# Logits of a graph network on Trainium2: the six steps of a narrow matmul dealt to four column groups

## The chip, the cores and the metric

The kernel runs on one core of one Trainium2 chip. The metric is the device time of one execution in microseconds, the median of several runs. TensorE (PE) does matmuls, VectorE (DVE) and ScalarE (ACT) work elementwise and empty PSUM, GpSimd (POOL) and SyncE (SP) mostly issue DMAs.

## What is computed

Four layers of a graph network over 512 nodes with 768 features and 8704 edges. Each layer adds a message-passing part, a mixing attention and a feed-forward part to the node features. Two kinds of stage matter here. The attention over edges needs, for each node, relation and head, two numbers (a query and a key logit):

```python
def rgat_conv(x, W, q, k, b, src, dst, etype, heads, out_ch, n_nodes):
    xr = jnp.einsum('nd,rdf->rnf', x, W)
    oi = xr[etype, dst]
    oj = xr[etype, src]
    qi = oi @ q
    kj = oj @ k
    alpha = jax.nn.leaky_relu(qi + kj, NEG_SLOPE)
    ...
```

with 3 relations, and 4 heads in the first of two such layers and 1 in the second; the last layer has an attention of 12 heads and one relation. The expert layers choose one of 8 experts for each node, by the largest of `_layernorm(x) @ Ws + bs`.

## The kernel before

Activations lie transposed: six chunks `[128 features, 512 nodes]` in SBUF, f32. A matmul contracts over 128 features, so that a product over 768 features is six steps (`KC = 6`) that accumulate in one PSUM bank. For the logits the stationary operand is narrow: `logit_w[heads]` has `2 * heads` columns (8, 2 or 24), and the gate of an expert layer 8 (`ME`). The result is `[2 * heads, 512]` in rows 0 up.

Every engine's program is written out by hand, in the order in which its queue runs. The engines meet by semaphores. PSUM's banks 0 to 3 form a ring: `open_bank` on TensorE waits until ScalarE (or VectorE) has emptied the bank four uses back, ScalarE empties the banks in the order in which they were filled (`filled`), and ticks `bank_free`. So a step that is moved on TensorE is moved on ScalarE too.

The stages around the change:

- `rgat` (TensorE, from L1200; ScalarE, from L1925; VectorE, from L2680), called for two layers, three relations each. For a relation: `linear` (36 matmuls with the relation's weights), `edge_logits` (the six narrow steps; ScalarE evicts them to `qkrow`, L1894), `to_tokens` (24 transposes of 128 x 128, six banks, evicted at L1578), `logit_columns` (four small transposes of `qkrow`), and `edge_softmax_row`, which spreads a key row over 128 partitions by a matmul with `key_of`. That last matmul waits for VectorE's `split_keys` (L2669 to L2676, five operations), which splits the f32 keys into three bf16 parts. ScalarE then adds query and key (L1920). For the third relation `to_tokens` comes after all of this, and the first exponentials (L1941) wait for VectorE's row maximum over all three relations.
- `graph_attention` (L1332): the six steps are followed by `res(0)`, which waits for the normalised features (`ln6`, L2282), then `logit_columns` and two rows.
- `experts_of_one` (L990, twice): the six steps of the gate run on the centred, not yet scaled features, behind the sum of squares. ScalarE evicts `logit_rows` (L1810), VectorE multiplies them by `rstd` (L2476, `logit_x`), behind its reciprocal (L2276), and four matmuls with an identity turn them into columns.

`stat` is a small scratch tile, `ident` the 128 x 128 identity.

## Time and profile before

| | |
|---|---|
| median of 3 runs | 4366.4 us (4365.52 to 4368.17) |
| the profiled execution | 4363.68 us, its span 4362.0 us |
| mean granted TensorE clock | 0.981 |
| busy: PE, DVE, ACT | 4137.1, 1153.9, 951.3 us |

The profile shows one execution. A TensorE instruction stands in two rows, PE (the matmul) and PEld (the load of its stationary operand). An f32 matmul is two records of each. A timeline row merges equal instructions: start, duration from the first start to the last end, count, and in brackets how long the engine sat idle before it and what released it.

### The profile page before, as it was taken

How to read it: one execution, taken by the hardware profiler on the slowest of the kernel's cores; microseconds unless marked ns; L12 is line 12 of the kernel's file. 1: busy time of each engine (PE TensorE's matmuls, PEld its weight loads, DVE VectorE, ACT ScalarE, POOL GpSimd, SP SyncE). 2: the span in 40 equal slices, each digit the busy share in tenths (PEclk: the TensorE clock that was granted, in tenths of full speed). 3: DMA queues.
4: the chain of work that ended last, by engine and by line, in shares of the span. 5: the costliest groups of instructions: out<-in, count | busy, mean ns of one | idle time of the engine just before them, and what ended most of it. 6: DMA issues, size and time to landing. Idle time of an engine off the chain costs nothing.

```text
span 4362.0 us, 37147 instructions
## 1 busy us (share of the span) xinstructions
PE 4137.1 (95%) x14783; PEld 1958.6 (45%) x14801; DVE 1153.9 (26%) x2082; ACT 951.3 (22%) x1743; POOL 137.5 (3%) x220
## 2 busy tenths in 40 slices
PE   8999999999999988989999999988999999999998
PEld 5444444444445444444454545434444333343333
DVE  7884221213221425113410111215530000000000
ACT  2121112434224336222200000116420100111000
POOL 2022000000000000000000000000000000000000
PEclk9999999999999999999999999999999999999999
DMA  5945422110741210103212122390159999999998
GB/s 194 295 138 155 122 85 80 37 44 22 288 186 44 68 58 1 61 27 134 72 55 92 61 84 69 128 368 25 53 205 424 406 422 416 423 423 404 424 410 358
DMA packets 170561, 802.34 MB, mean 184 GB/s; under 512 B 51898, under 2 KB 69114, under 8 KB 123812
## 3 DMA queue, kind: packets, MB, share of 16 engines
q1 hardware_dynamic: 158356, 733.39, 44.6%
q0 software_dynamic: 9584, 47.06, 2.8%
q10 hardware_dynamic: 2464, 19.67, 1.1%
q8 instruction: 115, 1.88, 0.2%
q14 instruction: 42, 0.34, 0.0%
HBM read 780.91 MB, written 71.10 MB: 195 GB/s over the span
## 4 chain that ended last, share of the span: by engine, by line
PE 83%; DMA 6%; DVE 5%; ACT 4%; issue 1%; POOL 0%; SPq 0%; DVEq 0%; ACTq 0%; POOLq 0%
PE bank L714 76%; DMA mem<-in_experts 4%; PE bank L875 3%; PE bank L712 2%; PE bank L849 1%; DMA mem<-moe_up 1%; ACT mem L1920 1%; DVE mem L2611 0%; ACT mem L1956 0%; ACT mem L1941 0%; ACT mem L2093 0%; DVE mem L2607 0%; DVE mem L2389 0%; DVE mem L2388 0%; DVE mem L2282 0%
## 5 line engine op out<-in xcount | busy, mean ns | idle before, releaser
L714 PE MATMUL bank<-mem 128*128 128x512 f32 (+4 forms) x10296 | 3161.8, 553 | 56.5 <-DMA mem<-in_experts 25.5
L714 PEld LDWEIGHTS bank<-mem 128*64 128x64 f32 (+2 forms) x10296 | 1330.8, 166 | 1788.2 <-issue 1675.6
L712 PE MATMUL bank<-ident,mem 128*128 128x128 f32 (+2 forms) x1484 | 228.7, 304 | 76.6 <-ACT mem L2120 14.8
L712 PEld LDWEIGHTS bank<-ident,mem 128*128 128x128 f32 (+2 forms) x1484 | 188.8, 157 | 169.6 <-issue 88.0
L1553 ACT ACTIVATE mem<-bank,cols 128x512 f32<-128x512 f32 x66 | 45.3, 687 | 760.7 <-PE bank L714 760.7
L875 PE MATMUL bank<-mem 128*128 128x512 bf16 x798 | 177.9, 382 | 3.5 <-DVE mem L2389 2.5
L2990 DVE TENSOR_TENSOR mem<-mem,EV 128x512 f32<-128x512 f32 x48 | 33.2, 692 | 550.0 <-ACT EV L2194 550.0
L2968 DVE TENSOR_TENSOR mem<-mem,bank 128x512 f32<-128x512 f32 x48 | 33.0, 688 | 456.3 <-PE bank L714 456.3
L714 PE MATMUL bank<-mem,ones 128*128 128x512 f32 (+1 forms) x290 | 128.3, 611 | 17.7 <-ACT mem L1587 7.2
L875 PEld LDWEIGHTS bank<-mem 128*128 128x128 bf16 x816 | 79.7, 98 | 101.4 <-DVE mem L2389 4.2
L1553 ACT ACTIVATE mem<-bank 128x512 f32<-128x512 f32 x81 | 47.7, 596 | 248.8 <-PE bank L714 244.0
L2194 ACT ACTIVATE EV<-bank 128x512 f32<-128x512 f32 x48 | 28.7, 597 | 307.4 <-PE bank L714 307.4
L2190 ACT ACTIVATE mem<-bank 128x512 f32<-128x512 f32 x48 | 28.7, 597 | 304.7 <-PE bank L714 304.7
L1564 ACT ACTIVATE EV<-bank,cols 128x512 f32<-128x512 f32 x30 | 20.6, 687 | 310.8 <-PE bank L714 310.8
L714 PEld LDWEIGHTS bank<-mem,ones 128*128 128x128 f32 (+1 forms) x290 | 50.1, 186 | 84.5 <-issue 53.4
L2871 DVE COPY mem<-mem 128x512 f32<-128x512 f32 x12 | 4.2, 421 | 307.8 <-ACT mem L1553 307.8
L714 PE MATMUL bank<-count_bits,row_first 128*128 128x512 f32 x288 | 79.9, 401 | 5.4 <-DVE row_rest L2853 5.4
L2389 DVE TENSOR_SCALAR mem<-mem 128x512 bf16<-128x512 f16 x204 | 84.7, 415 | 0.0
L2295 DVE TENSOR_TENSOR mem<-mem,EV 128x512 f32<-128x512 f32 x30 | 20.8, 692 | 230.7 <-ACT EV L1564 230.7
L849 PE MATMUL bank<-feat_hot,feat_bits 128*128 128x512 f32 x272 | 66.6, 404 | 15.5 <-DVE feat_bits L2336 15.5
L714 PE MATMUL bank<-count_bits,row_rest 128*128 128x512 f32 x288 | 79.6, 400 | 0.0
L2388 DVE TENSOR_SCALAR mem<-mem 128x512 bf16<-128x512 f16 x204 | 72.9, 357 | 20.8 <-PE bank L875 18.0
(401 smaller groups left out, 2560.9 us busy)
## 6 DMA issues: line engine op xcount, KB each, us to landing
mem<-in_experts SPq DMA_DIRECT2D x282, 1536.0 KB, 12.0
mem<-in_weights SPq DMA_DIRECT2D x285, 512.0 KB, 3.5
mem<-moe_up SPq DMA_DIRECT2D x30, 1152.0 KB, 9.6
mem<-moe_down SPq DMA_DIRECT2D x30, 1152.0 KB, 11.1
moe_up<-in_weights SPq DMA_DIRECT2D x16, 1152.0 KB
moe_down<-in_weights SPq DMA_DIRECT2D x16, 1152.0 KB
mem<-head_tiles SPq DMA_DIRECT2D x36, 384.0 KB, 3.0
mem<-in_weights POOLq DMA_DIRECT2D x36, 384.0 KB, 7.6
```

The lines of the kernel that those rows point to most:

```text
L712: ins = nc.tensor.transpose(out, lhsT, ident[0:lhsT.shape[0], 0:lhsT.shape[0]])
L714: ins = nc.tensor.matmul(out, lhsT, rhs, start=start, stop=stop)
L849: ins = nc.tensor.matmul(bank[4 + f][:, :], feat_bits[n % 3][:, part, at:at + P], feat_hot[:, n % 2 * 4 + b, :], start=n == 0 and b == 0 a ...
L875: ins = nc.tensor.matmul(banks[c][:, :], a[:, c * P:(c + 1) * P], b, start=False, stop=chunk == stop - 1)
L1553: nc.scalar.activation(dst(m), src[0:width, :], func, scale=scale, **how).then_inc(bank_free.sem, bank_free.tick((label, m)))
L1920: ins = nc.scalar.activation(scores[:, buf, t, :], src[:, :], ACT.Identity, bias=stat[:, at:at + 1])
L2190: nc.scalar.activation(x_hidden[:, b, :], src[:, :], ACT.Silu).then_inc(bank_free.sem, bank_free.tick((kind, p, b)))
L2194: nc.scalar.activation(EV[:, b % 2, :], src[:, :], ACT.Identity).then_inc(bank_free.sem, bank_free.tick((kind, p, b)))
L2388: v.tensor_scalar(onehot_a[:, done % AHEAD, :], iota_h, key(a, c), None, ALU.is_equal)
L2389: v.tensor_scalar(onehot_b[:, done % AHEAD, :], iota_h, key(b_, c), key(2 + p, c), ALU.is_equal, ALU.mult).then_inc(onehot_ready, 1)
L2968: v.tensor_tensor(XT[:, m, :], XT[:, m, :], bank[7][:, :], ALU.add).then_inc(dve_done.sem, dve_done.tick(("experts_x", p, m)))
L2990: v.tensor_tensor(x_hidden[:, u // 2, :], x_hidden[:, u // 2, :], EV[:, u // 2 % 2, :], ALU.mult).then_inc(dve_done.sem, dve_done.tick(("x ...
```

## The change

The six steps go to column groups 0, 1, 2, 3, 0, 1 of 32 columns each, so that steps 0 to 3 write to rows 0, 32, 64 and 96 of the bank, and steps 4 and 5 add to the first two. ScalarE evicts all 128 rows to `logit_rows`. `of_groups` is a matrix `[128, 32]` with a one where row and column agree modulo 32; a matmul with it adds the four groups. In the expert layers it takes the place of the identity in the four small matmuls; in the edge attentions it is a new step, `logit_sums`, with an eviction of its own. In `rgat` that step stands behind two of the six banks of `to_tokens`, in all three relations, and the third relation has two further banks ahead of `logit_columns`.

```diff
-        logit_rows = area(PQ_ + 6, 1, N, rows=ME)[:, 0, :]
+        logit_rows = area(PQ_ + 6, 1, N)[:, 0, :]
...
+        stat = sb("stat", [P, 256])
+        of_groups = stat[:, 224:256]
...
-            def to_tokens(label, source, ready=None):
+            def to_tokens(label, source, ready=None, part=range(KC)):
...
-                for n in range(KC):
+                for n in part:
...
                 for k in range(KC):
-                    ins = mm(out[0:ME, :], gate[:, k, :], centred[:, k, :], k == 0, k == KC - 1, k == KC - 1)
+                    at = 32 * (k % 4)
+                    ins = mm(out[at:at + ME, :], gate[:, k, :], centred[:, k, :], k < 4, k + 4 >= KC, k == KC - 1)
...
-                    pairs = [(logit_rows[:, t * P:(t + 1) * P], ident[0:ME, 0:ME])]
+                    pairs = [(logit_rows[:, t * P:(t + 1) * P], of_groups[:, 0:ME])]
...
-                    ins = mm(out[0:2 * heads, :], weights, source[:, j, :], j == 0, j == KC - 1, j == KC - 1)
-                ins.then_inc(bank_full.sem, bank_full.tick((tag, "qk", r)))
+                    at = 32 * (j % 4)
+                    ins = mm(out[at:at + 2 * heads, :], weights, source[:, j, :], j < 4, j + 4 >= KC, j == KC - 1)
+                ins.then_inc(bank_full.sem, bank_full.tick((tag, "qk_parts", r)))
+
+            def logit_sums(tag, heads, r):
+
+                out = open_bank()
+                pe.wait_ge(bank_free.sem, bank_free.at((tag, "qk_parts", r)))
+                mm(out[0:2 * heads, :], of_groups[:, 0:2 * heads], logit_rows, last=True).then_inc(
+                    bank_full.sem, bank_full.tick((tag, "qk", r)))
...
                     edge_logits(tag, heads, r, xr, after(bank_free, (tag, "xr", r)))
-                    if r < relations - 1:
-                        to_tokens((tag, "xr_tok", r), xr)
+                    to_tokens((tag, "xr_tok", r), xr, part=range(0, 2))
+                    logit_sums(tag, heads, r)
+                    to_tokens((tag, "xr_tok", r), xr, part=range(2, KC if r < relations - 1 else 4))
                     logit_columns(tag, heads, r)
                     edge_softmax_row(tag, heads, 0, r)
 
-                to_tokens((tag, "xr_tok", relations - 1), xr)
+                to_tokens((tag, "xr_tok", relations - 1), xr, part=range(4, KC))
...
                 res(0)
+                logit_sums(tag, heads, 0)
                 logit_columns(tag, heads, 0)
...
-                nc.scalar.activation(logit_rows, filled()[0:ME, :], ACT.Identity).then_inc(
+                nc.scalar.activation(logit_rows, filled()[:, :], ACT.Identity).then_inc(
...
-                v.tensor_tensor(logit_rows, logit_rows, rstd[0:ME, :], ALU.mult).then_inc(dve_done.sem, dve_done.tick((tag, "logit_x")))
+                v.tensor_tensor(logit_rows, logit_rows, rstd[:, :], ALU.mult).then_inc(dve_done.sem, dve_done.tick((tag, "logit_x")))
...
+            v.tensor_tensor(of_groups, ident[:, 0:32], ident[:, 32:64], ALU.add).then_inc(dve_done.sem, dve_done.tick())
+            for g in (2, 3):
+                dve.wait_ge(dve_done.sem, dve_done.now())
+                v.tensor_tensor(of_groups, of_groups, ident[:, 32 * g:32 * g + 32], ALU.add).then_inc(dve_done.sem, dve_done.tick())
```

ScalarE's program has the same order: its `edge_logits` evicts `[128, 512]` to `logit_rows`, its new `logit_sums` evicts to `qkrow`.

TensorE's order around the third relation of the first relation layer, before (`logit_w` are the six steps, `ident` with 128x4 the columns, `key_of` the row; row by row, with the number of equal instructions behind):

```order
L714 MATMUL bank<-mem 128x512 x36
L714 MATMUL bank<-mem,logit_w 8x512 x6
L712 MATMUL bank<-ident,mem 128x4 x4
L714 MATMUL bank<-mem,key_of 128x512
L712 MATMUL bank<-ident,mem 128x128 x40
```

The same place in the changed kernel (`of_groups` is part of `stat`; lines are one further down):

```order
L715 MATMUL bank<-mem 128x512 x36
L715 MATMUL bank<-mem,logit_w 8x512 x6
L713 MATMUL bank<-ident,mem 128x128 x8
L715 MATMUL bank<-mem,stat 8x512
L713 MATMUL bank<-ident,mem 128x128 x8
L713 MATMUL bank<-ident,mem 128x4 x4
L715 MATMUL bank<-mem,key_of 128x512
L713 MATMUL bank<-ident,mem 128x128 x24
```

Sixteen of the 24 token transposes now stand ahead of the row matmul, and the sum among them. (The 40 and 24 transposes at the end hold 16 of the next stage.) ScalarE at the same place, changed kernel; L1906 is the eviction of the parts, L1590 the tokens, L1911 the sums, L1916 the columns, L1937 the score additions:

```order
L1906 ACTIVATE mem<-bank 128x512
L1590 ACTIVATE mem<-bank 128x512 x2
L1911 ACTIVATE mem<-bank 8x512
L1590 ACTIVATE mem<-bank 128x512 x2
L1916 ACTIVATE stat<-bank 128x16
L1937 ACTIVATE mem<-bank,stat 128x512 x4
L1590 ACTIVATE mem<-bank 128x512 x2
```

Before, the eviction of the logits (8x512), of the columns and the additions followed one another, with all six tokens behind.

## Rows read from the trace of the kernel before

**Rows 1.** The page's chain that ended last, by engine.

```profile
PE 83%; DMA 6%; DVE 5%; ACT 4%; issue 1%; POOL 0%; SPq 0%; DVEq 0%; ACTq 0%; POOLq 0%
```

**Rows 2.** Groups by form, narrow matmuls: busy us, mean ns | idle before.

```profile
L714 PE MATMUL bank<-mem,logit_w 128*8 128x512 f32 x36 | 15.9, 592 | 0.0
L714 PE MATMUL bank<-mem,L_Ws 128*8 128x512 f32 x24 | 10.6, 593 | 0.0
...
L714 PEld LDWEIGHTS bank<-mem,logit_w 128*8 128x8 f32 x36 | 3.0, 90 | 12.4 <-issue 12.4
```

**Rows 3.** Timeline, first relation of the first relation layer: start us, us.

```profile
1522.80 5.32 PE L714 MATMUL bank<-mem,logit_w 128*8 128x512 f32 x12
1522.90 0.60 ACT L1553 ACTIVATE mem<-bank 128x512 f32<-128x512 f32 x1 [4.55 <-PE bank L714]
...
1528.04 3.18 PE L712 MATMUL bank<-ident,mem 128*128 128x128 f32 x28
1528.15 0.59 ACT L1894 ACTIVATE mem<-bank 8x512 f32<-8x512 f32 x1 [4.65 <-PE bank L714]
1528.74 3.04 ACT L1578 ACTIVATE mem<-bank 128x512 f32<-128x512 f32 x6
...
1530.76 0.68 DVE L2676 TENSOR_TENSOR mem<-mem 8x512 bf16<-8x512 f32 x1
1531.59 0.38 PE L714 MATMUL bank<-mem,key_of 96*128 96x512 bf16 x1 [0.37 <-DVE mem L2676]
```

**Rows 4.** Chain that ended last, third relation of that layer.

```profile
1611.46 0.60 PE bank L714
...
1612.09 2.43 ACT mem L1920 x4
```

**Rows 5.** Timeline: matmuls on two groups of 32, of 64, and one whole.

```profile
938.99 1.05 PE L714 MATMUL bank<-mem,ones 96*32 96x512 f32 x4
...
1145.80 4.09 PE L714 MATMUL bank<-mem 128*64 128x384 f32 x24 [0.48 <-ACT mem L1791]
...
1104.64 1.02 PE L714 MATMUL bank<-mem 128*128 128x512 f32 x2
```

**Rows 6.** Timeline, ahead of the logits' use in both expert layers.

```profile
1115.91 3.35 DVE L2276 RECIPROCAL rstd<-rstd 128x512 f32<-128x512 f32 x1 [3.90 <-ACT rstd L1590]
...
1120.44 0.59 ACT L1810 ACTIVATE mem<-bank 8x512 f32<-8x512 f32 x1 [4.56 <-PE bank L714]
1121.12 0.68 DVE L2476 TENSOR_TENSOR mem<-mem,rstd 8x512 f32<-8x512 f32 x1 [1.86 <-ACT mem L1810]
...
2810.85 3.35 DVE L2276 RECIPROCAL rstd<-rstd 128x512 f32<-128x512 f32 x1 [3.90 <-ACT rstd L1590]
...
2816.06 0.68 DVE L2476 TENSOR_TENSOR mem<-mem,rstd 8x512 f32<-8x512 f32 x1 [1.86 <-ACT mem L1810]
```

**Rows 7.** Timeline, start of the last attention.

```profile
2964.88 5.33 PE L714 MATMUL bank<-mem,logit_w 128*24 128x512 f32 x12
...
2971.32 1.13 PE L714 MATMUL bank<-mem,res 128*128 128x512 f32 x2 [1.10 <-DVE mem L2282]
2972.37 0.41 PE L712 MATMUL bank<-ident,mem 12*128 12x12 f32 x4
...
2973.78 4.73 ACT L1920 ACTIVATE mem<-bank,stat 128x512 f32<-128x512 f32 x8 [0.60 <-PE bank L714]
```

**Rows 8.** Stretches: length, busy of PE, PEld, DVE, ACT, POOL, then granted clock, DMA.

```profile
1530.00:1540.00 10.00, 9.63 (x34) 4.84 (x32) 6.21 (x12) 4.88 (x10) 0.00 (x0) 1.00 0.09 16
1570.00:1580.00 10.00, 9.70 (x34) 4.90 (x32) 6.15 (x12) 4.88 (x10) 0.00 (x0) 1.00 0.09 18
...
1123.50:1129.50 6.00, 6.00 (x29) 5.77 (x29) 3.40 (x13) 3.40 (x6) 0.00 (x0) 0.50 0.32 134
```

**Rows 9.** Timeline of VectorE where the change adds its preparation.

```profile
310.35 1.13 DVE L2754 COPY stat<-stat 32x2 f32<-32x2 f32 x6
...
318.57 0.75 DVE L2762 SCALAR_TENSOR_TENSOR mem<-EV,cols,mem 128x512 f32<-128x512 f32 x1 [2.58 <-ACT mem L1553]
```

More of the change, by code:

```diff
@@ L257, in program @@
         key_of = sb("key_of", [96, 24], bf16)
-        stat = sb("stat", [P, 256])
         comb, gate_exp, by_expert = (sb(n, [P, NT, ME]) for n in ("comb", "gate_exp", "by_expert"))
@@ L1572, in ev_free, with to_tokens @@
                 ev_reader[n] = label
-            def to_tokens(label, dst):
+            def to_tokens(label, dst, part=range(KC)):
                 flat = dst.rearrange("p t f -> p (t f)")
-                for n in range(KC):
+                for n in part:
                     act.wait_ge(bank_full.sem, bank_free.now(1))
@@ L2110, in graph_attention @@
                 res(0)
+                logit_sums(tag, heads, 0)
                 logit_columns(tag, heads, 0)
```

11 lines of the change are left out of this document (8 added, 3 removed).

## Prediction, made before the changed kernel ran

> **What bounds the kernel now.** I read the chain that ended last first: 83% of the span is the TensorE itself [rows 1], so time leaves this kernel where the TensorE has less to do or waits less, and only there. Next, the narrow matmuls. Each set of six f32 matmuls stands as 12 records of 592 ns that start 0.43 us apart and take 5.32 us together [rows 2, 3], whether 8 columns of the array are used or 128. There are nine sets: three in each of the two relation layers, one in the last attention, one in each expert layer. All nine together are about 48 us, 1.1% of the span. What follows a set differs, so I read the timeline at three kinds of place.
>
> *Relation layers, six places.* At the first one [rows 3] the set starts at 1522.80, ScalarE starts its eviction (L1894) at 1528.15, VectorE then splits the keys in five operations up to 1531.44, and the row matmul (`key_of`) starts at 1531.59. 24 token transposes fill the TensorE meanwhile, so it idles 0.37 us only; but the end of this path is eviction, then VectorE, not the transposes. For the third relation the transposes come after the row matmul, and the chain runs through the same operations into the row matmul at 1611.46 and ScalarE's score additions [rows 4]. So at all six the time that counts runs **from the set's start to the eviction's start: 5.35 us** (1528.15 − 1522.80).
>
> *Expert layers, two places.* Two paths meet in `logit_x` (L2476): the logit rows, evicted from 1120.44, and the reciprocal of the standard deviation, which VectorE finishes at 1119.26 (1115.91 + 3.35) and in the second layer at 2814.20 [rows 6].
>
> *Last attention, one place.* The set runs from 2964.88 to 2970.21, but the next matmul, `res` at 2971.32, waits for VectorE's normalisation (the wait in its row) [rows 7]. The set is hidden here.
>
> **What the change costs and gives, part by part.**
>
> *The set itself.* The nearest rows are matmuls on different column groups [rows 5]. Two matmuls on two groups of 32 columns, four records, take 1.05 us from first start to last end; one alone, two records, takes 1.02. 24 records on two groups of 64 columns take 4.09 us with 384 elements each, 0.17 apiece; one pass of 384 elements would take 0.32 at the pace of rows 3 (0.43 for 512). So two groups do run side by side. Four groups at once no row shows. Bounds: all four overlap, then 1.05 for steps 0 to 3 and 0.86 for steps 4 and 5, which wait for their groups: **1.9 us**; only two at a time, three pairs: 1.05 + 2 × 0.86 = 2.8 us; none, 5.3 us. I take 1.9, since the pair of 32-column matmuls, the nearest row, costs 0.03 us more than one. Step 5 needs the sixth chunk, evicted at 1523.50 (1522.90 + 0.60), 0.7 us after the start [rows 3]; the second wave starts 0.86 after it, so it doesn't wait.
>
> The Trainium skill ("TensorE: Matmul & The Clock Gate", Part 3) gives 2.38 times for three packed matmuls of 32 columns and 512 elements; by that figure, as an estimate, the set would take some 2.2 us. No run here shows three at once.
>
> *Relation layers: the new step.* After the parts' last record (1.9) ScalarE evicts them, 0.03 + 0.59: ready at 2.6 after the start. The TensorE has begun eight transposes at about 1.8 (they now start 0.1 before the set's end) and needs 0.9 for them (3.18 / 28 each [rows 3]): 2.7. So the wait for the parts is covered, with 0.1 us to spare. The sum is one f32 matmul, 1.02 us from first start to last end [rows 5]: 3.8. ScalarE has two token evictions of 0.5 behind the parts (3.04 / 6 [rows 3]), done at 3.7, so its eviction of the sum starts at **3.85 instead of 5.35: 1.5 us earlier**. What comes after (VectorE's splitting, then the row matmul) keeps its length. ScalarE's four remaining token evictions fit under VectorE's 2.7 us; where they don't, they delay the score additions by a few tenths. Late next: the TensorE now idles some 1.3 us before the row matmul instead of 0.37, since its own work fell by 5.15 − 1.7 − 0.86 = 2.6 us and the path by 1.5 only. In the first two relations the next layer of 36 matmuls follows the row matmul at once and gains the 1.5; in the third, the chain of rows 4 does. 6 × 1.5 = **−9.0 us**.
>
> *Expert layers.* Nothing is added: the four small matmuls take the sum over the groups. The parts are ready about 3.4 us earlier, at 1117.7, and `logit_x` then waits for the reciprocal: it starts at 1119.3 instead of 1121.12, 1.8 earlier; in the second layer 2814.25 instead of 2816.06, 1.8 [rows 6]. Everything behind it (normalisation, ranks, the scatter of rows) hangs on it. **−3.6 us.** ScalarE and VectorE handle 128 rows where it was 8; a [128, 512] eviction in rows 3 takes 0.60 against 0.59 for 8 rows: nothing.
>
> *Last attention.* The parts are early and hidden. But `logit_sums` stands behind `res`, ahead of the columns: one more matmul (0.9) and its eviction (0.6), which the column transposes at 2972.37 must await, before ScalarE's scores at 2973.78 [rows 7]. The eviction of `res` fits into the matmul. **+1.5 us.**
>
> *Preparation.* Three dependent VectorE additions, at about 0.2 each (six small copies took 1.13 us), before a stretch in which VectorE idles 2.58 us for ScalarE [rows 9]: hidden; without that cover it would be 0.6.
>
> Sum: −9.0 − 3.6 + 1.5 = −11.1 us. The profiled execution took 4363.7 (span 4362.0), so 4352.6; that execution was 2.7 us below the median of the runs, 4366.4. Against the median: **4355.3 us**, −0.25%. A measurement of this kernel can tell about 0.2% (8.7 us) from no change, so the line to "faster" lies at 4357.7.
>
> **Rivals.**
>
> *Two groups at a time.* For it: no row has more than two. Against: nothing in those two rows hints at a limit. The set takes 2.8, each relation place gains 0.6, the experts still 1.8 each (the reciprocal decides there): −3.6 − 3.6 + 1.5 = −5.7: 4360.7. Chance 0.12.
>
> *Weight loads that don't overlap.* All six steps use the same 128 rows. If a load had to wait for running matmuls, the 12 loads of 90 ns [rows 2] would stand in line, 1.1 us per set: each relation place would gain 0.4, sum −2.4 − 3.6 + 1.5: 4361.9. Against it: four 32-column records incl. their loads took 1.05 us in all [rows 5]. Chance 0.04. The Trainium skill states this rule in the same Part 3 (loads overlap running matmuls only when the row group differs); by it, this is the time, and rows 5 speak against it.
>
> *No overlap at all: slower.* If more than two groups, or groups that share one PSUM bank in two rounds, run one after another, the set keeps 5.3 us, and the new transposes' share (0.9) and the sum (1.0) stand on the path: +1.9 at six places, nothing at the experts, +1.5 in the last attention, +12.9: 4379. It decides when a set takes more than 3.4 us (5.35 − 1.9) in the relation layers. Rows 5 speak against it: the pairs there also share a bank. Chance 0.04.
>
> *The clock eats it.* In the first two relations the granted clock stays at 1.00 through the set and its transposes (2.4 GHz) [rows 8]. The change leaves a longer thin stretch there: 3.4 us of transposes, one sum, 1.3 us of idling. Where the TensorE did little, the clock fell to 0.50 (1.2 GHz) for 6 us [rows 8]; 6 us of dense matmuls at half clock lose 3. At all four places that is +12 and gives 4367, no change. For it: the longer idling. Against: 24 transposes in 3.2 us held the clock. Chance 0.09. The Trainium skill (same page, Part 4) says that transposes don't count as busy in the way matmuls do, which would favour this; here the clock is still at 1.00 behind 24 of them [rows 8], so the trace lends it no support. In the expert layers the clock is at 0.50 during the row transposes now [rows 8] and will be again; 24 transposes at half clock take twice their 2.6 us, so with the moment at which it falls up to 2.6 us per layer may come or go.
>
> **The numbers.** Forecast 0.71, rivals 0.12, 0.04, 0.04, 0.09. The forecast's own spread is some ±3 us (the clock in the expert layers, the overlap of waits); a part of it, about an eighth, lies above 4357.7. Faster by over 0.2%: 0.61. Within 0.2%: 0.1 from the forecast, 0.12 + 0.04 + 0.09 from rivals: 0.35. Slower: 0.04. Range 4351 to 4363: from the forecast with 4 us of clock luck to the two rivals of partial overlap with a little bad luck; outside it lie the serial case and most of the clock case.
>
> **What would show it.** Right: 12 records of a set within 2 us, four starting together; the second eviction (`qkrow`) 3.8 to 3.9 us after the set's start; the row matmul 8.8 − 1.5 = 7.3 us after the set's start; `logit_x` directly behind the reciprocal; `res` to scores 1.5 us longer. Wrong: records in pairs, or 0.43 apart; a clock of 0.50 at the start of the layers that follow the first two relations; the row matmul waiting for ScalarE rather than VectorE.

## The result, and the profile after

The changed kernel takes 4356.2 us (median of 9 runs, 4352.1 to 4363.5), the kernel before, on the same chip, 4366.4 (9 runs, 4362.8 to 4373.0). The ratio is 0.9978, 95% interval 0.9969 to 0.9986: 10.2 us faster, 6 to 14 by the interval. The forecast was 4355.3. The profiled execution took 4363.0 (span 4361.3), so it is one of the two slowest of the nine, and its first edge set starts 3.5 us later than before, behind code that the change hardly touches (the first expert set, the first place that the change touches, already starts 3.8 us later, at 1118.92 instead of 1115.08). So the reading goes by stretches, not by the span, and e5 gives a second profiled execution of the same kernel.

The chain by engine, to hold against [rows 1], in the changed kernel:

```profile
PE 84%; DMA 6%; DVE 4%; ACT 4%; issue 1%; POOL 0%; SPq 0%; DVEq 0%; ACTq 0%; POOLq 0%
```

The narrow matmuls by form, against [rows 2] (busy us, mean ns of one | idle before):

```profile
L715 PE MATMUL bank<-mem,logit_w 128*8 128x512 f32 x36 | 5.7, 594 | 0.0
...
L715 PE MATMUL bank<-mem,stat 128*8 128x512 f32 x6 | 3.1, 594 | 0.0
```

15.9 us of the first layer's sets became 5.7, and 3.1 us of sums are new. One record still takes 594 ns; it is that they lie beside each other. The first relation of the first layer, against [rows 3] (start, us):

```profile
1526.29 0.12 PEld L715 LDWEIGHTS bank<-mem,logit_w 128*8 128x8 f32 x8 [0.76 <-issue]
1526.30 1.89 PE L715 MATMUL bank<-mem,logit_w 128*8 128x512 f32 x12
...
1528.12 1.09 PE L713 MATMUL bank<-ident,mem 128*128 128x128 f32 x8
1528.23 0.60 ACT L1906 ACTIVATE mem<-bank 128x512 f32<-128x512 f32 x1 [1.23 <-PE bank L715]
...
1529.14 1.02 PE L715 MATMUL bank<-mem,stat 128*8 128x512 f32 x2
...
1530.20 0.59 ACT L1911 ACTIVATE mem<-bank 8x512 f32<-8x512 f32 x1 [0.30 <-PE bank L715]
...
1533.64 0.38 PE L715 MATMUL bank<-mem,key_of 96*128 96x512 bf16 x1 [1.25 <-DVE mem L2695]
```

Read it from the set's start, 1526.30. Eight weight loads, for four column groups and both passes of a step, are issued within 0.12 us, and all 12 records are over after 1.89. The parts' eviction starts at +1.93, the sum at +2.84, its eviction (L1911) at +3.90, the row matmul at +7.34 instead of 8.79. TensorE waits 1.25 us ahead of it, for VectorE (L2695).

In the third relation of that layer the chain runs as in [rows 4]:

```profile
1610.62 0.60 PE bank L715
...
1611.24 2.43 ACT mem L1937 x4
```

The row matmul is 7.28 us behind its set here (1603.34), 8.72 before (1611.46 behind 1602.74).

The expert layers, against [rows 6]:

```profile
1119.75 3.35 DVE L2295 RECIPROCAL rstd<-rstd 128x512 f32<-128x512 f32 x1 [5.60 <-ACT rstd L1602]
...
1120.86 0.60 ACT L1822 ACTIVATE mem<-bank 128x512 f32<-128x512 f32 x1 [1.14 <-PE bank L715]
1123.14 0.69 DVE L2495 TENSOR_TENSOR mem<-mem,rstd 128x512 f32<-128x512 f32 x1
...
2810.00 3.35 DVE L2295 RECIPROCAL rstd<-rstd 128x512 f32<-128x512 f32 x1 [3.90 <-ACT rstd L1602]
2813.39 0.69 DVE L2495 TENSOR_TENSOR mem<-mem,rstd 128x512 f32<-128x512 f32 x1
```

The parts are evicted from 1120.86 on, and `logit_x` (L2495) starts 0.04 us behind the reciprocal's end, in both layers, without a wait of its own in the row. Before, it waited 1.86 us for ScalarE.

The last attention, against [rows 7]:

```profile
2962.38 3.86 PE L715 MATMUL bank<-mem,logit_w 128*24 128x512 f32 x12
...
2963.39 0.12 PEld L715 LDWEIGHTS bank<-mem,logit_w 128*24 128x24 f32 x2 [0.48 <-DVE mem L2308]
...
2968.81 2.07 PE L715 MATMUL bank<-mem,res 128*128 128x512 f32 x2 [2.57 <-DVE mem L2301]
2970.82 1.73 PE L715 MATMUL bank<-mem,stat 128*24 128x512 f32 x2
...
2972.58 0.59 ACT L1911 ACTIVATE mem<-bank 24x512 f32<-24x512 f32 x1 [1.06 <-PE bank L715]
...
2974.69 4.74 ACT L1937 ACTIVATE mem<-bank,stat 128x512 f32<-128x512 f32 x8 [0.75 <-PE bank L715]
```

The set takes 3.86 us here and not 1.89, at a granted clock of 1.00: its steps wait for VectorE (L2308), which finishes a chunk every 0.60 us. From the set's start to `res` it is 6.43 us, as before: the set is hidden. But `res` now takes 2.07 us (1.13 before) and the sum 1.73 (1.02 at full clock): the granted clock is at half through `res` and part of the sum (0.71 on average from `res` to the scores). From `res` to the scores it is 5.88 us instead of 2.46.

The third relation of the *second* layer has no row in the section ahead of the prediction, since I had looked at the first layer's only. TensorE there, in the kernel before:

```profile
1885.44 0.59 PE L714 MATMUL bank<-mem,key_of 96*128 96x512 bf16 x1 [2.27 <-DVE mem L2676]
...
1896.91 3.65 PE L712 MATMUL bank<-ident,mem 128*128 128x128 f32 x16 [5.65 <-issue]
1903.07 3.93 PE L712 MATMUL bank<-ident,mem 128*128 128x128 f32 x32 [2.51 <-ACT mem L1956]
...
1908.48 30.71 PE L714 MATMUL bank<-mem 128*128 128x512 f32 x71 [0.50 <-ACT mem L1956]
```

and in the changed kernel:

```profile
1880.27 0.58 PE L715 MATMUL bank<-mem,key_of 96*128 96x512 bf16 x1 [2.06 <-DVE mem L2695]
1880.65 1.91 PE L713 MATMUL bank<-ident,mem 128*128 128x128 f32 x8
1891.75 3.65 PE L713 MATMUL bank<-ident,mem 128*128 128x128 f32 x16 [9.18 <-issue]
1897.91 6.58 PE L713 MATMUL bank<-ident,mem 128*128 128x128 f32 x32 [2.52 <-ACT mem L1974]
```

The row matmul starts 5.17 us earlier on the clock of the trace, the 32 transposes too (1897.91 against 1903.07). Then they take 6.58 us where they took 3.93, and the layer's output matmuls start at 1905.44 against 1908.48: 2.1 of the 5.2 us are gone. (Of the 5.2, this execution had 3.7 already at the set's start; 1.45 were gained between set and row matmul.) The stretches show why. Before (length, busy of PE, PEld, DVE, ACT, POOL, granted clock, DMA):

```profile
1885.00:1909.00 24.00, 14.89 (x83) 12.94 (x84) 6.84 (x19) 20.39 (x47) 0.00 (x0) 0.73 0.00 0
```

and after:

```profile
1880.00:1906.00 26.00, 13.98 (x67) 12.67 (x68) 6.67 (x19) 19.01 (x43) 0.00 (x0) 0.54 0.00 0
```

The change moved 16 token transposes from behind the row matmul to ahead of it. TensorE then sits idle 9.18 us for ScalarE's exponentials (which wait for VectorE's row maximum) instead of 5.65, and the clock is at 1.2 GHz nearly all the way through the 32 transposes, where before it was at 2.4.

In the first two relations, where my rival had put such a loss, the clock stays up behind the row matmul. Changed kernel, against [rows 8]:

```profile
1534.00:1544.00 10.00, 10.00 (x25) 4.42 (x24) 4.83 (x9) 3.02 (x5) 0.00 (x0) 1.00 0.16 52
1573.00:1583.00 10.00, 10.00 (x24) 4.37 (x23) 4.83 (x9) 2.72 (x6) 0.00 (x0) 1.00 0.18 52
```

The preparation, against [rows 9]:

```profile
310.81 0.19 DVE L2769 TENSOR_TENSOR stat<-ident 128x32 f32<-128x32 f32 x1
311.03 0.42 DVE L2772 TENSOR_TENSOR stat<-stat,ident 128x32 f32<-128x32 f32 x2
...
320.19 0.75 DVE L2785 SCALAR_TENSOR_TENSOR mem<-EV,cols,mem 128x512 f32<-128x512 f32 x1 [1.91 <-ACT mem L1565]
```

0.64 us of additions, and VectorE's wait behind them is 1.91 instead of 2.58: hidden.

### The profile page after: what moved, and what is told of

Its sections match the earlier page's. It is cut to its first block, busy times and chain, and to the rows that moved or that the text cites. A ratio compares the mean times of both kernels' runs of the same rounds, so it can differ in the third digit from the quotient of the medians.

```text
span 4361.3 us, 37192 instructions
## 1 busy us (share of the span) xinstructions
PE 4126.1 (95%) x14797; PEld 1953.6 (45%) x14815; DVE 1155.4 (26%) x2085; ACT 956.7 (22%) x1750; POOL 137.4 (3%) x220
## 4 chain that ended last, share of the span: by engine, by line
PE 84%; DMA 6%; DVE 4%; ACT 4%; issue 1%; POOL 0%; SPq 0%; DVEq 0%; ACTq 0%; POOLq 0%
PE bank L715 76%; PE bank L876 4%; DMA mem<-in_experts 4%; PE bank L713 3%; PE bank L850 1%; DMA mem<-moe_up 1%; ACT mem L1937 1%; ACT mem L1959 0%; ACT mem L2111 0%; DVE mem L2630 0%; DVE rstd L2295 0%; DVE mem L2626 0%; ACT mem L1974 0%; DVE mem L2301 0%; DVE node_rest L2794 0%
## 5 line engine op out<-in xcount | busy, mean ns | idle before, releaser
L1576 ACT ACTIVATE EV<-bank,cols 128x512 f32<-128x512 f32 x30 | 20.6, 687 | 311.3 <-PE bank L715 311.3
L850 PE MATMUL bank<-feat_hot,feat_bits 128*128 128x512 f32 x272 | 67.8, 408 | 15.9 <-DVE feat_bits L2355 15.9
## 6 DMA issues: line engine op xcount, KB each, us to landing
mem<-moe_down SPq DMA_DIRECT2D x30, 1152.0 KB, 10.7
```

Source lines behind the costliest of these rows:

```text
L850: ins = nc.tensor.matmul(bank[4 + f][:, :], feat_bits[n % 3][:, part, at:at + P], feat_hot[:, n % 2 * 4 + b, :], start=n == 0 and b == 0 a ...
```

## Experiments

All ratios are to the kernel before, measured on the same chip as the run, with 95% intervals. Their width is about 0.1% to either side, or 4 us, so effects of a few us are read from the traces, by three stretches that start and end at rows of TensorE:

- **period**: start of the first relation's edge set to that of the second, first relation layer;
- **relations**: start of the first edge set to the start of the second expert layer's set. Both relation layers lie in it, and some 900 us of matmuls that the change doesn't touch;
- **attention**: start of the last attention's set to the first matmul with the last gate's weights (`L3_gate`).

| profiled execution | median us | ratio (interval) | period | relations | attention |
|---|---|---|---|---|---|
| before | 4366.4 | 1 | 40.0 | 1287.2 | 243.3 |
| changed | 4356.2 | 0.9978 (0.9969 to 0.9986) | 38.6 | 1282.9 | 245.7 |
| e1 experts only | 4367.1 | 0.9992 (0.9983 to 1.0001) | 40.0 | 1287.2 | 240.5 |
| e2 relations only | 4360.2 | 0.9976 (0.9965 to 0.9987) | 38.6 | 1279.3 | 240.5 |
| e3 one group, with the sum | 4380.4 | 1.0021 (1.0012 to 1.0030) | 42.0 | 1300.9 | 239.9 |
| e4 two groups | 4364.1 | 0.9984 (0.9975 to 0.9993) | 39.4 | 1283.3 | 244.6 |
| e5 changed, again | 4360.6 | 0.9981 (0.9971 to 0.9990) | 38.6 | 1279.9 | 243.8 |
| e6 no sum in the attention | 4353.7 | 0.9961 (0.9947 to 0.9974) | 38.6 | 1282.9 | 235.1 |
| e7 filler in the wait | 4360.8 | 0.9983 (0.9974 to 0.9992) | 38.6 | 1279.4 | 242.8 |
| e8 no sums, no splits | 4344.3 | 0.9945 (0.9931 to 0.9959) | 37.2 | 1272.5 | 233.9 |
| e9 sum ahead of res | 4358.7 | 0.9976 (0.9967 to 0.9986) | 38.6 | 1280.5 | 242.3 |
| e10 rows of 128 | 4355.2 | 0.9971 (0.9962 to 0.9980) | 38.6 | 1280.8 | 236.7 |
| e11 e8 with filler | 4344.8 | 0.9939 (0.9923 to 0.9955) | 37.2 | 1272.8 | 240.3 |
| e12 e8 on one group | 4367.3 | 0.9990 (0.9980 to 1.0000) | 40.6 | 1294.0 | 240.3 |

Before and changed stand with the medians of the first comparison. The kernel before had medians of 4370.3, 4367.7 and 4369.3 us beside the three groups e1 to e4, e5 to e8 and e9 to e12, so only ratios are compared across groups.

### Parts of the change by themselves

**e1, experts only.** The edge sets, the sums and the order of the transposes are as before; the experts keep four groups.

```diff
-                    at = 32 * (j % 4)
-                    ins = mm(out[at:at + 2 * heads, :], weights, source[:, j, :], j < 4, j + 4 >= KC, j == KC - 1)
+                    ins = mm(out[0:2 * heads, :], weights, source[:, j, :], j == 0, j == KC - 1, j == KC - 1)
```

> Column groups in the two expert layers alone; relation layers and last attention as in the kernel before. My theory: the logit rows come 3.4 us earlier, logit_x then waits for the reciprocal, 1.8 us earlier per layer: -3.6 us. A first look at the changed kernel's trace has a rival: in the first expert layer the eight small matmuls with the bias took 3.03 us instead of 2.47 (8 rows became 128), so -1.2 there and -3.0 in all. If the experts give nothing because the clock falls earlier: 0. All three are near what this measurement can tell, so the verdict is read from the stretch from the set's start to the ranks: 1.8 us (theory) or 1.3 us (rival) shorter in the first layer.

Ratio 0.9992, or 3.5 us of 4370: what was expected, though the interval reaches past 1 and alone shows no gain. The trace does. `logit_x` starts 4.21 us behind the set instead of 6.04, the full 1.8, in e1 and in the changed kernel. But in the first expert layer the four small matmuls with their bias now take longer, 3.03 us in the changed kernel instead of 2.47. Before:

```profile
1121.86 0.38 PE L714 MATMUL bank<-ident,mem 8*128 8x8 f32 x2 [1.46 <-DVE mem L2476]
...
1124.33 5.45 PE L712 MATMUL bank<-ident,mem 128*128 128x128 f32 x24
```

and in the changed kernel:

```profile
1123.88 0.39 PE L715 MATMUL bank<-stat,mem 128*128 128x8 f32 x2 [3.07 <-DVE mem L2495]
...
1126.91 5.38 PE L713 MATMUL bank<-ident,mem 128*128 128x128 f32 x24
```

At full clock the pairs of small matmuls stand 0.31 us apart, before 0.22. From the set's start to the transposes it is 7.99 us in the changed kernel and 8.12 in e1, against 9.25: 1.3 and 1.1 gained there. Two later executions with the same code, e11 and e12, take 9.15, with the clock at half through all of the small matmuls, so the gain in the first layer is not safe either. In the second layer, without a bias, the eight records take 1.06 us where they took 1.05, and from the set to the transposes it is 5.88 us instead of 7.76 in both: 1.9 gained.

**e2, relations only.** The last attention keeps one group and no sum, and the experts are as before.

```diff
-                    at = 32 * (k % 4)
-                    ins = mm(out[at:at + ME, :], gate[:, k, :], centred[:, k, :], k < 4, k + 4 >= KC, k == KC - 1)
+                    ins = mm(out[0:ME, :], gate[:, k, :], centred[:, k, :], k == 0, k == KC - 1, k == KC - 1)
```

> Column groups and the sum in the two relation layers alone; experts and last attention as in the kernel before. Theory: six places at 1.5 us, -9.0 us. Rival (the longer stretch at clock 0.50 behind the third relation of the second relation layer, 23.9 us instead of 13.7): five places at 1.45, the sixth gives back 2.1 in its 32 transposes: -6.6 us. In the trace: the sets of one layer 38.5 us apart instead of 40.0 either way; clock 0.50 through the transposes of the weights in the rival.

Ratio 0.9976, or 10.5 us, with 5.7 to 15.3 by the interval: it holds both 9.0 and 6.6 and doesn't decide. The trace does, in part. The period is 38.6. The whole stretch gains 7.9 us, where the changed kernel's first profiled execution, with the same code there, had gained 4.3. Most of their difference arises behind the third relation's set of the second layer: from it to the second expert set it is 933.3 us before, 933.9 in e2 and 936.2 in the changed kernel. Up to the layer's output matmuls it is 31.8 us before, 31.0 in e2 and 32.4 in the changed kernel, so e2 does gain 0.8 at the place; it loses 1.4 in the 900 us behind, which the change doesn't touch.

### The size of the set

**e3, one group, with the sum.** All six steps of an edge set go to rows 0 on; the parts' eviction and the sum stay, with the identity in place of the ones and zeros.

```diff
-                    at = 32 * (j % 4)
-                    ins = mm(out[at:at + 2 * heads, :], weights, source[:, j, :], j < 4, j + 4 >= KC, j == KC - 1)
+                    ins = mm(out[0:2 * heads, :], weights, source[:, j, :], j == 0, j == KC - 1, j == KC - 1)
...
-                mm(out[0:2 * heads, :], of_groups[:, 0:2 * heads], logit_rows, last=True).then_inc(
+                mm(out[0:2 * heads, :], ident[:, 0:2 * heads], logit_rows, last=True).then_inc(
```

> The changed kernel with all six steps of the edge sets on one group of 32 columns again (experts keep their four groups); the parts' eviction and the sum stay. It prices the added step. My prediction's serial case: +1.9 us at six places against the kernel before, experts -3.6, last attention +1.5: +9.3 us, ratio about 1.002. If the step costs less than I worked out (the sum hidden behind transposes and VectorE): second eviction less than 7.25 us after the set's start and a total near 0 or below. In the trace: set 5.3 us, second eviction 7.25 us after its start.

Ratio 1.0021, which is the serial case of the prediction (+12.9 us) with the experts' 3.6 taken off: +9.3 us of 4370. The period is 41.98 us, 1.97 over before. TensorE at the first relation:

```profile
1523.49 5.32 PE L715 MATMUL bank<-mem,logit_w 128*8 128x512 f32 x12
1528.74 1.09 PE L713 MATMUL bank<-ident,mem 128*128 128x128 f32 x8
1529.76 1.02 PE L715 MATMUL bank<-mem,ident 128*8 128x512 f32 x2
...
1534.27 0.38 PE L715 MATMUL bank<-mem,key_of 96*128 96x512 bf16 x1 [1.25 <-DVE mem L2694]
```

So the added step costs 2.0 us at each of the four places with a next relation behind them, 1.9 expected, and it is on the path. At the third relations it comes out unevenly, 0.4 us from the third set to the next layer's first in the first layer (194.5 against 194.1) and 5.4 to the second expert set in the second (938.7 against 933.3), where the clock is at half for longer.

**e4, two groups,** in the experts too; the matrix then takes one addition instead of three.

```diff
-                    at = 32 * (j % 4)
-                    ins = mm(out[at:at + 2 * heads, :], weights, source[:, j, :], j < 4, j + 4 >= KC, j == KC - 1)
+                    at = 32 * (j % 2)
+                    ins = mm(out[at:at + 2 * heads, :], weights, source[:, j, :], j < 2, j + 2 >= KC, j == KC - 1)
```

> The changed kernel with two groups of 32 columns instead of four, in all nine sets. Theory (what counts is how many groups run side by side): set 1.05 + 2 x 0.86 = 2.8 us, each relation place gains 0.6 us instead of 1.5, experts unchanged since the reciprocal decides there: 5.4 us slower than the changed kernel, about 0.9988 of the kernel before. Rival (four groups gain through something else, for instance that steps to one group no longer stand behind each other in pairs): two groups take 1.9 us as well and the time is that of the changed kernel. If two groups of 32 do not overlap over a run of six: 5.3 us.

Ratio 0.9984, expected 0.9988. The pairs stand one after another as worked out, 2.75 us instead of 2.8:

```profile
1522.76 2.75 PE L715 MATMUL bank<-mem,logit_w 128*8 128x512 f32 x12
```

The set's length is the number of rounds on one group (6, 3, 2) times 0.86 us and a tail of 0.17, wherever its input is ready: 5.32, 2.75, 1.89. In the last attention, where the steps wait for VectorE, two groups take 3.86 us as four do.

### The last attention, and the clock

**e5, the changed kernel again,** with no edit.

> The changed kernel itself, unchanged, as a companion of the next three on the same chip and as a second profiled execution. Expected ratio to the kernel before 0.9977 (between 0.9969 and 0.9986, its first interval). From the first edge set to the second expert set its first profiled execution took 4.4 us less than the kernel before, the run with the relation layers alone 8.0 us less with the same code there: if the moments at which the clock falls make that difference, this execution lies somewhere between 4 and 9 us again.

Ratio 0.9981. The relations stretch gains 7.4 us this time (4.3 in the first profile). Over the six executions that have the changed relation layers (changed, e2, e5, e6, e9, e10) the gain is 4.3, 7.9, 7.4, 4.3, 6.7 and 6.4: 6.2 on average, against 9.0 forecast. The traces divide it. Each cell has the length and, in brackets, the part of it at half clock, in us:

| | first layer, third set to output matmuls | from there to the next layer's first set | second layer, third set to output matmuls | from there to the second expert set |
|---|---|---|---|---|
| before, e1 | 35.0 (17) | 159.1 (17) | 31.8 (14) | 901.5 (17) |
| the six | 33.3 to 33.5 (17 to 24) | 157.7 to 159.2 (3 to 17) | 31.0 to 32.5 (17 to 24) | 902.8 to 903.8 (20) |

The four places with a next relation behind them gain 1.45 each, 5.8. The third of the first layer gains 1.4 to 1.7 up to its output matmuls, as forecast. The third of the second layer gains 0.8 at best and loses 0.7 at worst, a loss of 0.2 on average. That makes 7.1 us at the six places. The stretches behind, with the same instructions as before, give 0.9 in the first layer and take 1.85 in the second.

**e6, no sum in the attention.** The parts stay in 128 rows and the columns and rows take them directly; in the relation layers nothing changes.

```diff
-                    key = ident[0:2 * heads, heads + h:heads + h + 1].to_broadcast([2 * heads, P])
-                    ins = mm(out[:, :], key, qkrow[0:2 * heads, r, :], last=True)
+                    key = of_groups[:, heads + h:heads + h + 1].to_broadcast([P, P])
+                    ins = mm(out[:, :], key, gat_rows, last=True)
```

> The changed kernel, but in the last attention the sum goes: the row and column matmuls take the matrix of ones and zeros and all 128 rows of parts as their operands, so one matmul and one eviction less stand behind res. My prediction's theory: 1.5 us faster than the changed kernel there. Rival from the changed kernel's first trace (TensorE waits 2.57 us ahead of res, the clock is at 0.50 from res on, res to scores 5.88 us instead of 2.46): 2.4 to 3.4 us faster there if the clock stays up, and res to scores back to 2.5 us; if the clock still falls, res to scores about 3.5. Read from the trace, since the total can't tell 1.5 from 3.

Ratio 0.9961, and the attention is 10.7 us shorter than in the changed kernel's first profile, 8.7 than in its second. That is more than either theory, and not at the place that I had named: `res` to the scores still takes 5.3 us, at half clock. The rest of the gain lies further down the attention.

**e7, filler.** Ten f32 matmuls of 512 columns that feed nothing, in the wait for the exponentials in the second relation layer.

```diff
+                if tag == "rgat2":
+                    for n in range(FILL_SCORES):
+                        mm(bank[4][:, :], ones[:, :], xr[:, 0, :])
```

> The changed kernel with ten f32 matmuls of 512 columns (8.6 us at full clock) that feed nothing, put in the second relation layer where TensorE waits 9.2 us for ScalarE's exponentials. Theory (the low clock behind that wait costs the 32 transposes and eight small matmuls 7.5 us instead of 5.4): they take 5.4 again, 2.1 us faster than the changed kernel there, clock 1.00 through them. Rival: the clock falls all the same, nothing gained; or the added matmuls run at half clock (17 us) and stand in the way: 8 us slower.

TensorE there:

```profile
1876.28 8.75 PE L716 MATMUL bank<-mem,ones 128*128 128x512 f32 x20
1886.46 1.94 PE L714 MATMUL bank<-ident,mem 128*128 128x128 f32 x16 [1.43 <-issue]
1892.62 5.38 PE L714 MATMUL bank<-ident,mem 128*128 128x128 f32 x32 [4.22 <-ACT mem L1978]
```

The clock holds for the 16 transposes (1.94 us instead of 3.65), which is no use, since they wait for ScalarE's evictions either way, and falls in the middle of the 32. From the set's start to the output matmuls it is 31.0 us against 32.4 and 31.9 in the two profiles of the changed kernel: 0.9 to 1.4 us shorter. But e2, with the same relation layers and no filler, takes 31.0 as well, and its 32 transposes take 5.38 us too, so the run doesn't show that the filler gave anything back. The total doesn't show it either (0.9983).

**e9, the sum ahead of res**, on TensorE and ScalarE alike.

```diff
+                logit_sums(tag, heads, 0)
                 all_of(dve_done, "ln6")
                 res(0)
-                logit_sums(tag, heads, 0)
```

> The changed kernel with the sum of the last attention ahead of res on TensorE and ScalarE, where it falls into the 2.57 us that TensorE waits for VectorE. Theory (the sum costs what stands on the path there): res to scores 2.5 us again at full clock, where it was 5.88 (clock 0.50) in the changed kernel and 4.24 at full clock in the run with one group: 1.8 us faster, and up to 3.4 if the earlier sum also keeps the clock up. Rival: the run without the sum gained 8 us in the last attention for another reason, namely that its rows come from 128 rows instead of 24 (low clock there 20 us instead of 34 to 41); then this run gains its 1.8 and no more, and from the set to the last gate's matmuls it stays above 240 us.

TensorE and, behind it, the first scores:

```profile
2963.50 1.02 PE L715 MATMUL bank<-mem,stat 128*24 128x512 f32 x2 [0.78 <-ACT mem L1906]
2965.29 1.13 PE L715 MATMUL bank<-mem,res 128*128 128x512 f32 x2 [0.77 <-DVE mem L2301]
```

```profile
2967.76 4.74 ACT L1937 ACTIVATE mem<-bank,stat 128x512 f32<-128x512 f32 x8 [0.60 <-PE bank L715]
```

The sum fits into the wait: `res` still starts 6.43 us after the set, and the scores follow 2.47 us after it, as before the change. At full clock the sum behind `res` had cost 1.8 (e3: 2984.01 to 2988.25, 4.24), at half clock 3.4 and 4.1 (5.88, and 6.57 in e5). The half clock doesn't come with the order alone: in e4 and e10, with the sum behind `res` and the same wait ahead of it, the clock stays up and it is 4.24 and 4.35. The attention as a whole is 242.3 us in e9, so by this one execution the rival was right that e6 gained by something else.

**e10, rows of 128.** The sum stays behind `res`; the row matmuls of the attention read 128 rows, of which 24 count.

```diff
-                    key = ident[0:2 * heads, heads + h:heads + h + 1].to_broadcast([2 * heads, P])
-                    ins = mm(out[:, :], key, qkrow[0:2 * heads, r, :], last=True)
+                    key = ident[:, heads + h:heads + h + 1].to_broadcast([P, P])
+                    ins = mm(out[:, :], key, gat_rows, last=True)
```

> The changed kernel, the sum kept where it is, but the row matmuls of the last attention read all 128 rows (24 of them meet a one or a zero that counts, the others zeros) instead of 24. No instruction is added or removed and the work per matmul in columns is the same. Theory A (the height of the operands matters to the clock): low clock in the last attention about 20 us instead of 34 to 41, from the set to the last gate's matmuls some 238 to 240 us instead of 243 to 246. Theory B (the moments at which the clock falls are luck): as the changed kernel, 243 to 246.

The attention takes 236.7 us, on theory A's side and below its 238 to 240, and the granted clock over it is 0.97:

```profile
2956.25:3192.99 236.74, 212.38 (x767) 103.86 (x766) 122.07 (x305) 123.76 (x266) 4.92 (x8) 0.97 0.17 54
```

In the changed kernel it is 0.92:

```profile
2962.38:3208.12 245.74, 225.67 (x767) 106.64 (x766) 122.09 (x305) 123.98 (x266) 4.93 (x8) 0.92 0.17 52
```

But e11 and e12 read 128 rows too, without a sum, and stand at 240.3 us. e11:

```profile
2951.41:3191.72 240.31, 220.07 (x769) 108.61 (x769) 122.09 (x305) 123.18 (x265) 4.95 (x8) 0.93 0.17 53
```

So theory A doesn't hold as I put it. Over all executions the attention takes 237.3 us on average with rows of 128 (e6, e8, e10, e11, e12) and 242.6 without (nine); each of the nine has the clock at 0.92 to 0.96. Of the difference, about 1.1 us is plain: at full clock the next matmul starts 1.05 us behind the start of a row matmul with 24 rows, and 0.86 to 0.96 behind one with 128, twelve times. The rest goes with the clock for the most part. But e1 has the attention of the kernel before, word for word, and takes 240.5 us against 243.3; and with five executions whose values lie between 233.9 and 240.3 I leave open how much is the rows' height and how much the moment.

### Without the sum

**e8, no sums and no splits.** ScalarE evicts 128 rows of parts per relation; columns and rows take them in f32 with the ones and zeros; VectorE's five operations per relation go.

```diff
-                    ins = mm(out[:, t * heads:(t + 1) * heads], qkrow[0:heads, r, t * P:(t + 1) * P], None, last=t == NT - 1,
-                             transpose=True)
+                    ins = mm(out[:, t * heads:(t + 1) * heads], qkrow[:, r, t * P:(t + 1) * P], of_groups[:, 0:heads], last=t == NT - 1)
...
-                    pe.wait_ge(dve_done.sem, dve_done.at((tag, "key_bits", r)))
-                    key = key_of[:, heads + h:heads + h + 1].to_broadcast([96, P])
-                    ins = mm(out[:, :], key, key_bits[:, r, :], last=True)
+                key = of_groups[:, heads + h:heads + h + 1].to_broadcast([P, P])
+                ins = mm(out[:, :], key, qkrow[:, r, :], last=True)
```

In the first two relations the remaining transposes stand ahead of the row, in the third behind it.

> The changed kernel without the sum anywhere: ScalarE evicts all 128 rows of parts, the columns and the rows of all heads take them directly in f32 with the matrix of ones and zeros (columns: four f32 matmuls in place of four transposes), and VectorE's splitting of the keys into three parts (2.7 us) falls away. Worked out: in the first two relations of a layer TensorE has no wait left and is the bound: set 1.9 + 24 transposes 3.2 + columns 0.4 + row 1.0 = 6.5 us ahead of the next layer's matmuls, where it was 7.6: 1.1 us per place less; in the third the row stands right behind eight transposes, at 3.2 us after the set's start instead of 7.3, and takes 0.6 longer: 3.5 less; the rows of later heads in the first relation layer take 0.5 us more, three on the path: +1.5; last attention -1.5 to -3.4. Sum against the changed kernel 2 x (2 x -1.1 - 3.5) + 1.5 - 1.5 = -11.4 us, ratio to the kernel before about 0.995. Rival: VectorE and ScalarE (maxima, exponentials) are the bound behind the third relation and take it back, or the longer wait for them keeps the clock at 0.50: -4.4 - 1.5 = -6 only.

4344.3 us, ratio 0.9945 (expected about 0.995): the fastest kernel here together with e11, and faster than both kernels of the comparison. The period is 37.2 us (37.5 expected, 38.6 less 1.1). TensorE in the third relation of the first layer:

```profile
1596.87 1.89 PE L715 MATMUL bank<-mem,logit_w 128*8 128x512 f32 x12
...
1599.62 0.96 PE L715 MATMUL bank<-stat,mem 128*128 128x4 f32 x8
1600.43 1.10 PE L715 MATMUL bank<-mem,stat 128*128 128x512 f32 x2
```

The row stands 3.56 us after the set (3.2 expected; the columns take 0.8, not 0.4). In the first layer nothing is left of it in the end: from this set to the next layer's first it is 192.1 us, against 192.7 and 191.1 in the changed kernel's two profiles, since the rows of the later heads, now f32, cost 0.7 us per head or more (15.5 instead of 14.8 us from one head's transposes to its output matmuls). In the second layer, with one head, the row's gain stays: 27.96 us from the third set to the output matmuls against 32.4 and 31.9.

**e11, e8 with eight filler matmuls,** in the place of e7's.

```diff
+FILL_SCORES = 8
```

> The kernel without sums and splits, plus eight f32 matmuls that feed nothing in the second relation layer where TensorE waits 7.65 us for the exponentials. It tells whether clock that is held there is worth something at the end: the 32 transposes and eight sums took 6.3 us there (5.4 at full clock), the 16 before them 3.65 (1.94 at full clock, but they wait for ScalarE's evictions): -0.9 us. Rival: nothing, since ScalarE's exponentials decide. Not to be seen in the total either way; read from the trace.

28.04 us for the same stretch: nothing gained. The 16 transposes take 1.94 us instead of 3.65 but wait for ScalarE's evictions either way, and the 32 behind them take 5.35 as against 5.38 in e8, since the clock falls in them all the same. Ratio 0.9939, not to be told from e8.

**e12, e8 with one group.**

```diff
-                key = of_groups[:, heads + h:heads + h + 1].to_broadcast([P, P])
+                key = ident[:, heads + h:heads + h + 1].to_broadcast([P, P])
```

The set's own edit is that of e1.

> The kernel without sums and splits, but all six steps of the edge sets on one group of columns again (experts keep four groups; the rows then need no sum at all). It separates what column groups are worth from what leaving out the sum and VectorE's splitting is worth. Theory: each relation place gets 5.32 - 1.89 = 3.4 us longer, 20.6 in all, the last attention hides its set: ratio to the kernel before 0.9945 + 0.0047 = 0.9992. Rival: without the split the set is hidden behind something else (ScalarE's evictions), then less than 10 us.

Ratio 0.9990 (expected 0.9992). The period is 3.4 us longer than in e8, and the relations stretch 21.5 us longer, for six sets of 3.43 us each: 20.6. But e12's relations stretch is also 6.8 us longer than that of the kernel before, with sets of the same length: f32 rows and columns over 128 rows, in place of the splits and with the order that goes with them, are a loss there by themselves (the period is 40.6 against 40.0). Against the kernel before, e8's relation layers gain 14.7 us, not 21.5.

## Why the prediction was right, and which steps of it were not

*The set: right.* 1.89 us for 1.9; the pair of [rows 5] was the row to go by, and the rule behind it holds at all three sizes (e3, e4). The rivals of partial overlap and of none are out; e3 and e4 build them and gave 1.0021 and 0.9984, where the prediction's sums make 1.0021 (with the experts' gain) and 0.9987. The Trainium skill ("TensorE: Matmul & The Clock Gate", Part 3) lets a weight load overlap running matmuls only when its row group differs. Here all loads are for the same 128 rows, eight of them stand in 0.12 us under the first running matmuls, and the set is as short as with no such rule: the trace disagrees with the rule in that form. In the kernel before, on one column group, a set's second load already starts at 1522.80, under the record that runs from 1522.80 to 1523.39. The same Part also speaks of a background weight buffer into which loads may go ahead; that would allow both, and no run here tests it. By the figure of the Trainium skill (same Part) for three packed matmuls I had estimated 2.2 us; 1.89 was measured.

*Relation layers, first two relations: right.* The second eviction starts 3.90 us after the set (3.85 forecast), the row 7.34 (7.3), TensorE idles 1.25 us (1.3), and a period is 1.45 us shorter (1.5). Two small sums of mine don't close: 2.7 + 1.02 and the 0.03 to 0.05 of a start make 3.75, not 3.85 (the sum in fact starts at 2.84), and 0.37 + 2.6 - 1.5 makes 1.5 us of idling, not 1.3.

*Relation layers, third relation: the step that failed, in the second layer.* I wrote that "in the third, the chain of rows 4 does" gain the 1.5. In the first layer it does: 1.4 to 1.7 us up to the output matmuls. In the second the 1.45 are gained up to the transposes (26.36 us from the set before, 24.91 in the changed kernel), and between there and the output matmuls it is 7.5 us instead of 5.4, with the clock at half over the 32 transposes; over six executions the place gives -0.2 us on average instead of 1.5. Six places: 7.1 us instead of 9.0. The stretches behind, which the change doesn't touch, lose another 0.9 net, which makes the 6.2: with them the first layer's third set is 192.7, 191.4, 191.1, 192.7, 191.1 and 191.0 us from the next layer's first, against 194.1, and the second layer's third set 933.9 to 936.2 us from the second expert set, against 933.3. The clock was among my rivals, but at the first two relations, where it stays at 1.00; I had looked at the places that get thinner by idling and not at the one from which the change takes 16 transposes away. That these transposes are the cause is argued and not shown: no run puts only them back. The traces are in keeping with it. TensorE idles 5.7 us there before and in e1, with 13.7 us at half clock up to the output matmuls; it idles 9.2 to 10.0 in the changed order (the six, e3, e4), with 17 to 24. In e8 and e12, with 16 of the 24 transposes behind the row, it idles 7.65, with 13.7.

*Experts: right in the mechanism, a little less in size.* `logit_x` stands directly behind the reciprocal. I wrote that "nothing is added"; the four small matmuls that alternate with a one-row bias matmul read 128 rows now and take 0.56 us more in the first layer, so it is 1.1 to 1.3 + 1.9, or 3.0 to 3.2, instead of 3.6, and 1.0 less where the clock falls ahead of them (e11, e12).

*Last attention: the place was right, the size was not.* +1.5 was worked out for a full clock: it is 1.8 to 1.9 there (e3, e4, e10), and 3.4 and 4.1 in the changed kernel's own two executions, where the clock is at half at this place in both. e9 takes it back by order alone.

*Preparation: right,* 0.64 us hidden.

The parts as measured make about -6.2 - 3.1 + 1.8 to 4.1, or -5 to -7.5 us, and the total -10.2 with an interval from 6 to 14 and -8.3 in the second comparison (4 to 13). So the median came out nearer to my sum than the parts would have it, and that 4356.2 is so close to 4355.3 is in part luck. -7.5 lies in both intervals, -5 in the second alone. The total alone could not have shown that the third relation and the attention had been taken wrongly; only the stretches do.

What the change is worth is plainer from e3 and e12. The column groups save 3.4 us at each of six places, some 20 us; the sum takes 1.9 of each back, 11 us, and the clock another 2 to 3. Once the consumers add the groups up themselves, the whole amount shows against the same kernel on one group (e8 against e12, 21.5 us), and 14.7 against the kernel before.

## What to carry to other kernels

Splitting a sum over column groups leaves partial rows that have to be added, and where the next consumer is itself a matmul it can do that with a matrix of ones and zeros for little (0.4 us for the columns, 0.7 per later head for f32 rows in place of bf16 ones, 0.6 in the first expert layer); a step of its own costs a matmul and an eviction on the path (1.9 us here), more than half of what the groups give. Before placing small work, look at where TensorE idles on both sides: with the transposes moved ahead of the row the next wait was longer, and the clock stayed low for longer behind it. The same sum was free ahead of a wait, and cost 2 to 4 us behind it. And measure stretches between fixed rows as well as the total, since a profiled execution of the same code differed by 3.6 us in one of them.

## What the runs showed of the hardware

- Four f32 matmuls on four groups of 32 columns run side by side at no cost: rounds of 0.86 us (512 columns, two passes) whether a round holds one, two or four groups (e3, e4, the changed kernel), with outputs in one bank and loads for the same rows.
- At full clock the next matmul starts 1.05 us behind the start of an f32 row matmul with 24 rows (two passes, before), and 0.86 to 0.96 behind one with 128 rows (e8).
- Where the clock falls differs between executions of one kernel, and moves 2 to 4 us in a stretch of 1280: e5 against the changed kernel, 1279.9 and 1282.9 us for the same code. Low clock that lies over TensorE's waits or over transposes that wait for ScalarE costs nothing (16 transposes in 3.65 or 1.94 us, same end); over the 32 transposes ahead of dense matmuls it costs up to 2.1 us (5.4 us from their start to the output matmuls before, 7.5 in the changed kernel).
